# Splitting one wait for sixteen constants into five, and moving the expert weights and zero rows into the attention pipeline

## What is computed

```python
x = x + attn(layernorm(x), Wq, Wk, Wv, Wo, q_gain, pair_mix)
x = x + ffn(layernorm(x), router_w, w_gate, w_up, w_down)
```

## Time and profile before

| | us |
|---|---|
| median of 3 runs | 601.63 |
| lowest and highest | 601.54, 603.01 |
| the profiled execution, its own time | 603.13 |
| its span, first to last instruction | 601.3 |
| TensorE busy | 531.7 (88%) |
| VectorE busy | 446.0 (74%) |
| ScalarE busy | 332.9 (55%) |
| GpSimd busy | 337.1 (56%) |

### The profile page before, as it was taken

How to read it: one execution, slowest core, us unless ns; L and a number is a source line. 1 busy time by engine, 2 the same in 40 slices (tenths; PEclk the granted TensorE clock), 3 DMA queues, 4 the chain that set the end, 5 groups by cost and what they waited for, 6 DMA issues and landing times. The chain is left out here.

```text
span 601.3 us, 20442 instructions
## 1 busy us (share of the span) xinstructions
PE 531.7 (88%) x6060; PEld 382.0 (64%) x6060; DVE 446.0 (74%) x1764; ACT 332.9 (55%) x1171; POOL 337.1 (56%) x468
## 2 busy tenths in 40 slices
PE   0599999899999999999984799999999999999970
PEld 0267787677777777777763466666666666666650
DVE  2569999999999999999999455646565555656553
ACT  1446776667767667767653455454544455444530
POOL 1222221866668766668754748264655655557655
PEclk9999999999999999999998599999999999999995
DMA  9512211332223322212231223244655554554543
GB/s 304 186 36 45 46 28 37 73 68 63 58 66 75 71 52 48 51 55 59 57 84 49 76 85 119 76 132 130 164 140 142 146 141 136 143 147 132 150 112 86
DMA packets 123530, 58.06 MB, mean 97 GB/s; under 512 B 53793, under 2 KB 118689, under 8 KB 123169
## 3 DMA queue, kind: packets, MB, share of 16 engines
q1 hardware_dynamic: 112640, 34.90, 23.6%
q0 software_dynamic: 8192, 16.79, 9.9%
q10 hardware_dynamic: 2592, 5.07, 2.2%
HBM read 28.14 MB, written 24.64 MB: 88 GB/s over the span
## 5 line engine op out<-in xcount | busy, mean ns | idle before, releaser
L1205 POOL DMA_INDIRECT expert_in<-xn,slot_r x128 | 127.5, 996 | 88.5 <-DVE slot_r L837 64.4
L1274 POOL DMA_INDIRECT ga<-expert_out,row_all x128 | 122.2, 954 | 92.4 <-DVE yb L1168 30.4
L653 PE MATMUL chb<-wgu,xbT 128*128 x288 | 151.1, 607 | 0.0
L1161 DVE TENSOR_TENSOR h<-sil,chb 128x256 f32<-128x256 f32 x144 | 60.6, 421 | 102.3 <-ACT sil L466 102.2
L381 ACT ACTIVATE pT<-chb 128x512 f32<-128x512 f32 x128 | 76.5, 598 | 83.6 <-DVE mx L854 49.2
L466 ACT ACTIVATE sil<-chb 128x256 f32<-128x256 f32 x144 | 55.4, 384 | 121.4 <-PE chb L653 121.4
L667 PEld LDWEIGHTS chb<-ident,h 128*128 128x128 f32 x288 | 40.5, 142 | 79.0 <-issue 42.5
L854 DVE TENSOR_REDUCE mx<-chb 128x8 f32<-128x512 f32 x128 | 85.4, 676 | 2.6 <-PE chb L577 2.1
L667 PE MATMUL chb<-ident,h 128*128 128x128 f32 x288 | 55.6, 275 | 1.5 <-DVE h L1161 1.4
L1229 POOL TENSOR_TENSOR tq<-t,rr 128x128 f32<-128x128 f32 x64 | 27.0, 421 | 48.7 <-issue 44.2
L596 PE MATMUL pp<-wp,xyT 128*128 128x272 f32 x128 | 50.2, 476 | 4.2 <-DVE t L939 2.6
(11 more groups left out here) (142 smaller groups left out, 1156.6 us busy)
## 6 DMA issues: line engine op xcount, KB each, us to landing
xb<-expert_in SPq DMA_DIRECT2D x144, 64.0 KB, 1.8
expert_out<-yb SPq DMA_DIRECT2D x72, 128.0 KB, 1.9
xa<-x SPq DMA_DIRECT2D x16, 256.0 KB, 3.1
out<-oo SPq DMA_DIRECT2D x32, 128.0 KB, 2.1
qk<-qk SPq DMA_DIRECT2D x64, 48.0 KB
wgu<-w_gu ACTq DMA_DIRECT2D x1, 2048.0 KB, 8.8
expert_in<-xn,slot_r POOLq DMA_INDIRECT x128
ga<-expert_out,row_all POOLq DMA_INDIRECT x128, 2.6
```

What stands on the lines that cost most here:

```text
L653: nc.tensor.matmul(chb[:, b % 2, :], xbT[:, b % 4, :], wgu[:, e, :], start=True, stop=True).then_inc(gu_done, 1)
L1161: nc.vector.tensor_tensor(h[:, b % 4, :], sil[:, b % 2, :], chb[:, b % 2, FF:2 * FF], ALU.mult).then_inc(h_ok, 1)
L1205: nc.gpsimd.indirect_dma_start(xs_dram, bass.IndirectOffsetOnAxis(ap=slot_r[:, q % 4, 2 * v + k:2 * v + k + 1], axis=0), xn2[:, t % 16, :] ...
L1274: nc.gpsimd.indirect_dma_start(ga[:, q % 2 * TPS + v, j, :], None, ys_dram[0:blocks * P, :], bass.IndirectOffsetOnAxis(ap=row_all[:, q * T ...
```

## The change

The sixteen constants are divided into five groups with a semaphore each. ScalarE keeps the identity and projection weights (`for_proj`) and the rope table and gains (`for_rope`). SyncE takes the other three groups, between its four loads of x. Each consumer waits for its own group where it first needs it: TensorE for `for_proj` at its start, for `for_mask` in step 9, for `for_out` in step 13, for `for_route` in step 20. VectorE scales `tab` after its step 3, mixes `wo` after step 9 and copies `base` after step 13. ScalarE copies `selr` after its step 6. SyncE loads `wgu` and `wdn` after the DMAs of its step 20 and writes the eight blocks of zeros after those of its step 23.

```diff
-MEM = 8
+MEM = 5
...
+        for_proj = ((ident, ident_in), (wp, w_proj))
+        for_rope = ((tab, rope), (gn, gain))
+        for_mask = ((eyes, eyes_in), (masks, masks_in), (selg, selg_in))
+        for_out = ((oneblk, oneblk_in), (wos, wo_self), (wop, wo_pair), (mixs, mix_self), (mixp, mix_pair))
+        for_route = ((wr, w_router), (tri, tri_in), (region, region_in), (cells, cells_in))
+
+        def load(eng, pairs, landed):
+            for dst, src in pairs:
+                eng.dma_start(dst[:], src).then_inc(landed, 16)
...
-            for q in range(4):
-                load_x(q)
-            sp.wait_ge(zero_ok, 1)
-            for n in range(SPARE):
-                sp.dma_start(xs_dram[EXP * CAP + n * P:EXP * CAP + (n + 1) * P, :], zero[:, :]).then_inc(c_zero, 16)
+            load_x(0)
+            load(sp, for_mask, c_mask)
+            load_x(1)
+            load(sp, for_out, c_out)
+            load_x(2)
+            load(sp, for_route, c_route)
+            load_x(3)
             for s in range(STEPS):
                 step(s)
+                if s == L_TX2:
+                    sp.dma_start(wgu[:, :, :], w_gu).then_inc(c_moe, 16)
+                    sp.dma_start(wdn[:, :, :, :], w_dn).then_inc(c_moe, 16)
+                if s == L_RANK:
+                    sp.wait_ge(zero_ok, 1)
+                    for n in range(SPARE):
+                        sp.dma_start(xs_dram[EXP * CAP + n * P:EXP * CAP + (n + 1) * P, :], zero[:, :])\
+                          .then_inc(c_zero, 16)
...
-            for dst, src in constants:
-                act.dma_start(dst[:], src).then_inc(c_attn, 16)
-            act.dma_start(wgu[:, :, :], w_gu).then_inc(c_moe, 16)
-            act.dma_start(wdn[:, :, :, :], w_dn).then_inc(c_moe, 16)
+            load(act, for_proj, c_proj)
+            load(act, for_rope, c_rope)
...
-            act.wait_ge(c_attn, CONSTS)
-            nc.scalar.copy(selr[:, :], selg[:, :]).then_inc(c_mem, 1)
             for s in range(S_MOE):
                 step(s)
+                if s == L_XT:
+                    act.wait_ge(c_mask, len(for_mask) * 16)
+                    nc.scalar.copy(selr[:, :], selg[:, :]).then_inc(selr_ok, 1)
...
-            pe.wait_ge(c_attn, CONSTS)
-            pe.wait_ge(c_mem, MEM)
+            pe.wait_ge(c_proj, len(for_proj) * 16)
...
+                if s == L_S:
+                    pe.wait_ge(c_mem, MEM)
+                    pe.wait_ge(c_mask, len(for_mask) * 16)
+                    pe.wait_ge(selr_ok, 1)
+                if s == L_PV:
+                    pe.wait_ge(c_out, len(for_out) * 16)
+                    pe.wait_ge(wo_ok, 1)
+                if s == L_RT:
+                    pe.wait_ge(c_route, len(for_route) * 16)
...
             for s in range(S_MOE):
                 step(s)
+                if s == TPS - 1:
+                    scale_rope()
+                if s == L_S:
+                    mix_out()
+                if s == L_PV:
+                    first_base()
```

More of the change, by code:

```diff
@@ L213, in kernel_body @@
         LG, PREF, TOT = P, P + TPS * EXP, P + 2 * TPS * EXP
-        c_attn, c_moe, c_mem, c_zero = (sem(n) for n in ("const_attn", "const_moe", "const_mem", "const_zero"))
+        c_proj, c_rope, c_mask, c_out, c_route = (sem("const_" + n) for n in ("proj", "rope", "mask", "out", "route"))
+        c_moe, c_mem, c_zero = (sem(n) for n in ("const_moe", "const_mem", "const_zero"))
+        tab_ok, selr_ok, wo_ok, base_ok = sem("tab_ok"), sem("selr_ok"), sem("wo_ok"), sem("base_ok")
         pads_ok, aligned_ok = sem("pads_ok"), sem("aligned_ok")
@@ L704, in _, with scale_rope, mix_out, first_base @@
             nc.vector.memset(both[:, :, :, :], 0.0).then_inc(c_mem, 1)
[L705 to L714, removed]
+            def scale_rope():
+                dve.wait_ge(c_rope, len(for_rope) * 16)
+                for u in range(TPS):
+                    for n in range(2):
+                        q_part = tab[:, u, n, :].rearrange("p (a x) -> p a x", a=2)[:, :, 0:QF // 2]
+                        last = nc.vector.tensor_tensor(q_part, q_part, gn[:, :, :], ALU.mult)
+                last.then_inc(tab_ok, 1)
+            def mix_out():
+                dve.wait_ge(c_out, len(for_out) * 16)
+                nc.vector.tensor_scalar(wor[:, :], wop[:, :], mixp[:, 0:1], None, ALU.mult).then_inc(wor_ok, 1)
+                dve.wait_ge(wor_ok, 1)
+                nc.vector.scalar_tensor_tensor(out=wo[:, :], in0=wos[:, :], scalar=mixs[:, 0:1], in1=wor[:, :],
+                                               op0=ALU.mult, op1=ALU.add).then_inc(wo_ok, 1)
+            def first_base():
+                dve.wait_ge(c_route, len(for_route) * 16)
+                nc.vector.tensor_copy(base[:, 0, :], region[:, :]).then_inc(base_ok, 1)
             first_slot = cells[:, 0:CELLS]
@@ L814, in ranks @@
                 before = base[:, q, :]
+                if q == 0:
+                    dve.wait_ge(base_ok, 1)
                 if q == SPLIT:
@@ L936, in step @@
                     dve.wait_ge(v_ok, t + 1)
+                    if t == 0:
+                        dve.wait_ge(tab_ok, 1)
                     wait(dve, t3_ok, t - 3)
```

## The result

| | median us | lowest, highest | runs | ratio to before, 95% interval |
|---|---|---|---|---|
| before | 601.63 | 599.82, 603.01 | 7 | |
| the change | 605.7 | 603.45, 608.33 | 7 | 1.0064 [1.0042, 1.0086] |

The change makes the kernel slower by 0.64%, some 4 us. The forecast was 599.4, with a range to 602.2. The profiled execution of the changed kernel took 603.67 us (span 601.9), so it is one of its quick ones, while the one of before was slow for its kernel; the two spans differ by only 0.6 us. The places of gain and loss are read from these traces, their size over many executions from the ratio.

A forecast was written before the change was run, and what follows sets the result against it. Attention steps were taken to have no slack, TensorE and VectorE being nearly always busy, so only time before step 6 could be won. The sum -7.6 + 0.7 + 2.6 + 2.1 = -2.2 us gave 599.4, range 596.8 to 602.2.

The forecast's parts named there:

- its three signs of being wrong: No idle time in step 22; `gn` landing later than 9; matmuls of doubled duration between 70 and 110 us.
- a fall of the clock, held at 0.16 as a rival: Stalls in steps 22 and 25 lower TensorE's clock once; two slower steps cost 1.6 us: 601.0; chance 0.16.
- The start: a gain: Start of the kernel: `gn` lands at 7.9, so `nb` runs 7.6 us earlier; bounds 6.8 and 9.2.
- The second rival: The start gives less (`gn` a microsecond later) or the weights' stall reaches its upper bound: 601.0; chance 0.20.
- the bound of 6.8: Start's lowest gain, if DMA engines at 322 GB/s first move all both queues hold, `gn` about 0.8 us later.
- What is put back inside the steps: Work moved into later steps (cast of `selr`, `wor` and `wo`, copy to `base`) costs 0.7 us (0.2 to 0.9).
- Weights after step 20: Step 22: key copies wait behind 3 MB in SyncE's queue, landing at about 83.5; a stall of 2.6 us.
- the bound of 4.2: Step 22's upper stall: `wdn` landing 10.9 us after an issue at 74.0, at 84.9.
- 3072 KB in 7.7 us, about 406 GB/s: Rate for the weights in step 20, from landings of `cells` (13.36) and `wdn` (21.1) before the change.
- Zeros after step 23: Step 25: eight zero writes delay x and tile 16's key copy; a stall of 2.1 us (1.4 to 3.0).
- Between the stalls lie two full steps, and at the head two such steps were enough for the rise: Argument against the clock staying low from step 22 on, a case of 604.3 with chance 0.07.
- the weights hold nothing up: Step 22: later small transfers pass the 3 MB, so the stall is gone: 596.8; chance 0.13.

The follow-up runs named there:

- the kernel with pieces: The changed kernel with weights and zeros each in eight pieces, issued after eight of SyncE's steps from 29 to 42; 593.98 us, ratio 0.9896 to before.
- the last one: The kernel with pieces, but SyncE issues two groups of x, then waits for the rope table and gains before its other loads; 592.09 us, ratio 0.9855.
- the moves only: The kernel before with weights moved after SyncE's step 20 and zeros after its step 23, one semaphore for all constants; 611.26 us, ratio 1.0173.
- the kernel with short rows in ScalarE's queue: The changed kernel with step 20's weights issued by ScalarE as four DMAs with rows of 2 and 1 KB; 603.91 us, ratio 1.0045.

## Why the prediction was wrong

The places, the waits and what ends them were right, and two of its three signs of being wrong came: `gn` landed after 9, and matmuls between 70 and 110 us took double time. The sizes of three terms of its sum were off, the largest that of the weights, and a fall of the clock, held at 0.16 as a rival, came in both stalls.

- **"The start: a gain", 7.6 us: measured 5.4.** The step that failed is "`gn` takes 5.7 us, so it lands at 7.9". I compared bytes on both queues and took them for equal. It took 8.1 us here and 7.7 in the kernel with pieces, which differs at the start from the last one only in SyncE's constants held back, with 4.8: those loads cost it 2.9 us. The second rival had this, but with one microsecond, and the bound of 6.8 was too narrow. (x's second group is the fifth load of SyncE, not the sixth; it did not bind.)
- **"What is put back inside the steps", 0.7: measured 0.1.** From TensorE's first transpose to its first scores pass 9.46 us (12.97 to 22.43) instead of 9.39 (18.38 to 27.77); the next step is 3.43 in both.
- **"Weights after step 20", 2.6: measured 5.9, beyond the bound of 4.2.** The failed term is "3072 KB in 7.7 us, about 406 GB/s", taken from the landing of `cells` to that of `wdn`. A distance of two landings is short where some DMA engines are into the second transfer before the last of the first has landed; that this is the reason is argued, not tested. From issue to landing the row of before had 10.9 us where I forecast 9.3 here; it was 11.8 us. Counted from the issue of x, `wdn` landed after 13.5 us (64.49 to 78.0) where the forecast has 10.9 (72.43 to 83.3), which is 2.7 of the 3.3 us missing. The trace also shows a tail: 393 and 377 GB/s from 70 to 74 us, 365 to 76, then 97, at a DMA share of 0.36. The keys, ordered behind all of it, are released only at 78.59.
- **"Zeros after step 23", 2.1: measured 2.1.**
- **The clock.** "Between the stalls lie two full steps, and at the head two such steps were enough for the rise" was right, so it did not stay low; but it fell in both stalls, for 1.5 and 1.4 us. The step that failed is leaving the fall out of the forecast because the 1.40 us wait of the earlier trace rows had left the clock alone: a wait of 2.60 us (step 25, with one of 0.84 shortly before it) was enough.

With the measured terms, -5.4 + 0.1 + 5.9 + 1.5 + 2.1 + 1.4 = +5.6. In this profiled execution the first rise of the clock also came a step sooner (steps 10 to 14 take 14.8 us, 25.86 to 40.63, instead of 16.8, 31.20 to 47.98), which makes +3.6, against +3.9 by the ratio. The forecast had this at nothing. It seems to come with the split: steps 10 to 14 take 14.6 to 15.6 us in eight of the nine traces of kernels that have it and 16.4 in the ninth, against 16.8 before and 16.3 with the moves only, one execution each. In the trace step 26 is only 2.7 us late (101.38 to 98.70), since another 0.8 is won from step 20 to step 21 (4.4 us instead of 5.2), where TensorE waited 1.12 us for ScalarE's `pT` before. Why the span ends only 0.6 us later is open: the rest is made up in later steps that run unevenly in both traces. The spread between executions of one kernel (599.8 to 603.0, 603.5 to 608.3) is as large.

The rival "the weights hold nothing up" was wrong in SyncE's queue and in ScalarE's. The one that did not get a place in the prediction was the dependence of the start's gain on the weights' move: alone, the split is worth nothing.

## What to carry to other kernels

Before moving a large load out of the way, look at what else stands in that queue and how soon it is wanted; in the same queue it waits for all that stands ahead, and from another queue it is held up as well (9.2 us instead of at most 3.6 here). And count steps before naming the transfer that a wait is for: the last one issued before the wait ends need not be it. In a pipeline without slack a load of 3 MB in one place costs its whole surplus and then the clock; the same load in eight pieces between the small transfers left no wait for keys over 1.3 us. Take a transfer's time from issue to landing under the load it will meet, not from the distance of two landings.

## What was not expected of the hardware

- A copy of 48 KB in rows of 512 B, issued by SyncE 0.1 us after ScalarE had issued 2 MB in another queue, was used 9.2 us after its issue; the same copy just ahead of the weights in their own queue, at most 3.6 us after. Beside the same bytes as four transfers with shorter rows it took 6.6 us.
- SyncE's issues themselves slowed at the start, 1.67 us for the 64 KB of `wos` and 1.49 for the 4 KB of `wr`, where most others take 0.43 to 0.60; why was not tried.
- A wait of TensorE of 2.60 us took its clock from 2.4 to 1.2 GHz; after work resumed at 95.73 it was back at full by about 99 us, and after the longer wait, resumed at 78.59, by 82. In the kernel with short rows in ScalarE's queue waits of 1.69 and 1.28 us, with 1.3 us of work between, were enough (0.96 from 70 to 72 us, 0.50 from 72 to 74), where before the one wait of 1.40 us was not.
